# Expert products and sums over both column halves at once, row scaling split between ScalarE and VectorE

## What is computed

```python
logits = x @ router_w + router_b
topk_vals, topk_idx = top_k(logits, 2)
full_w = sum(one_hot(topk_idx, 8) * softmax(topk_vals)[..., None], axis=-2)
h = einsum('td,edf->etf', xf, expert_w) + expert_b[:, None, :]     # 8 dense experts
combined = einsum('etf,te->tf', silu(h), full_w)
y = x + combined @ proj_w + proj_b
return norm_w * (y / sqrt(mean(y * y, -1) + 1e-6))
# around it: x = x + 0.5 * ffn(layernorm(x))
```

## Time and profile before

| | us |
|---|---|
| median of 3 runs | 890.74 |
| lowest, highest | 890.63, 891.22 |
| the profiled execution | 892.65 |
| its span, first to last instruction | 890.8 |
| TensorE (PE) busy | 822.6, 92% |
| VectorE (DVE) busy | 701.0, 79% |
| GpSimd (POOL) busy | 585.2, 66% |
| ScalarE (ACT) busy | 521.4, 59% |
| mean granted TensorE clock | 0.971 |

### The profile page before, as it was taken

The page is one execution under the profiler, slowest core; times in us unless marked ns, Lnnn a source line. Parts: engine busy times, 40 slices in busy tenths (PEclk is TensorE's granted clock), DMA queues, the critical chain, the costliest instruction groups (busy, mean ns, idle before and its releaser), DMA issues. The chain is left out here.

```text
span 890.8 us, 17017 instructions
## 1 busy us (share of the span) xinstructions
PE 822.6 (92%) x4848; PEld 724.0 (81%) x4848; DVE 701.0 (79%) x1824; ACT 521.4 (59%) x1252; POOL 585.2 (66%) x444
## 2 busy tenths in 40 slices
PE   5998888767999999999999999999999998999984
PEld 4776776656889999999999899899999986787873
DVE  6899989899776776776866867767767797789987
ACT  3654534445765765755865766756767663554542
POOL 3667746368587687777777787777777812556743
PEclk9999988978999999999999999999999999899998
DMA  8053153410212311312312312212212100000001
GB/s 302 1 178 105 72 201 142 142 36 12 49 24 59 106 24 35 94 35 59 94 24 47 94 24 71 85 33 47 71 41 54 25 1 29 1 1 24 24 1 47
DMA packets 26673, 55.98 MB, mean 63 GB/s; under 512 B 3568, under 2 KB 9840, under 8 KB 25104
## 3 DMA queue, kind: packets, MB, share of 16 engines
q1 hardware_dynamic: 26640, 55.59, 21.4%
HBM read 22.02 MB, written 12.58 MB: 39 GB/s over the span
## 5 line engine op out<-in xcount | busy, mean ns | idle before, releaser
L1050 POOL TENSOR_TENSOR at_ql<-at_rot,at_qh 128x512 fp32r<-128x512 f32 x62 | 79.8, 1287 | 99.6 <-ACT at_qh L1272 99.6
L1289 ACT ACTIVATE at_pr<-at_sm,at_low 128x512 f32<-128x512 f32 (+3 forms) x256 | 140.4, 555 | 0.9 <-DVE at_low L1137 0.8
L1295 ACT ACTIVATE at_pth<-at_pt 128x512 fp32r<-128x512 f32 (+1 forms) x192 | 95.8, 525 | 76.0 <-PE at_pt L1449 75.2
L603 ACT ACTIVATE f_s<-f_ex,f_cols 128x512 f32<-128x512 f32 x128 | 84.1, 686 | 86.0 <-PE f_ex L751 46.3
L293 POOL TENSOR_TENSOR f_acc<-f_acc,f_u 128x512 f32<-128x512 f32 x68 | 100.8, 1509 | 40.8 <-DVE f_u L482 27.7
L1147 DVE TENSOR_SCALAR at_pr<-at_pr,at_inv 128x128 f32<-128x128 f32 (+3 forms) x256 | 113.1, 504 | 2.3
L1137 DVE CUSTOM_DVE_ANT_0 at_sm<-at_sc,at_mask 128x512 f32<-128x512 f32 (+3 forms) x256 | 109.8, 484 | 2.5 <-issue 2.4
L1152 DVE TENSOR_TENSOR at_ptl<-at_pt,at_pth 128x512 fp32r<-128x512 f32 (+1 forms) x192 | 108.7, 593 | 1.7 <-ACT at_pth L1295 1.5
L1059 POOL TENSOR_TENSOR at_rot<-ga,cos 128x512 f32<-128x512 f32 x78 | 104.2, 1336 | 4.1 <-POOL at_ql L1050 2.4
L1065 POOL TENSOR_TENSOR at_rot<-at_rot,gc 128x512 f32<-128x512 f32 x78 | 101.5, 1301 | 8.1 <-POOLq L1082 2.1
L1449 PE MATMUL at_pt<-ident,at_pr 128*128 128x128 f32 x640 | 96.3, 278 | 9.3 <-DVE at_pr L1147 6.8
(11 more groups left out here) (212 smaller groups left out, 2262.7 us busy)
## 6 DMA issues: line engine op xcount, KB each, us to landing
gc<-ga SPq DMA_DIRECT2D x160, 128.0 KB, 2.3
ga<-in_attn_w SPq DMA_DIRECT2D x4, 1280.0 KB, 7.7
attn_split<-gb SPq DMA_DIRECT2D x4, 1280.0 KB, 9.6
attn_split<-gc SPq DMA_DIRECT2D x4, 1280.0 KB, 12.1
gb<-attn_split SPq DMA_DIRECT2D x8, 512.0 KB, 4.2
at_wo<-attn_split SPq DMA_DIRECT2D x8, 512.0 KB, 4.3
x<-in_x SPq DMA_DIRECT2D x4, 512.0 KB, 9.0
e_raw<-in_expert_w SPq DMA_DIRECT2D x8, 256.0 KB, 6.7
```

The costliest lines, as they stand in the source:

```text
L1289: act.activation(pr[h % 2][:, cols], sm[h % 2][:, cols], ACT.Exp, bias=low[h % 2][:, i:i + 1], scale=-1.0, accum_out=tot[h % 2][:, i:i + 1 ...
```

## The change

The rings `s_ring` and `u_ring` become two wide buffers of both halves each, with the same capacity. One product of 1024 columns (the bank of `w_ps` is read twice by a broadcast) takes the place of two, except for expert 7 of the last block. The pair sums, GpSimd's sums, the rounding of the sum and its rest become one operation each. The semaphores count up by two at once. Row scaling is divided: ScalarE multiplies each row by its inverse root mean square (four operations after silu of expert 3), VectorE then multiplies all four tiles by `norm_w` in one operation, after expert 4 and `z_rest`. GpSimd's `add_rows` moves from behind the sum of expert 3 to behind the pair of experts 4 and 5.

```diff
@@ -116,8 +116,8 @@
         fw = sb("fw", [P, BT, P])
         wT = sb("wT", [P, SEQ], F32R)
 
-        s_ring = [sb(f"s{n}", [P, SEQ]) for n in range(4)]
-        u_ring = [sb(f"u{n}", [P, SEQ]) for n in range(4)]
+        s_ring = [sb(f"s{n}", [P, C, SEQ]) for n in range(2)]
+        u_ring = [sb(f"u{n}", [P, C, SEQ]) for n in range(2)]
         acc = sb("acc", [P, C, SEQ])
         ch, cl = sb("ch", [P, C, SEQ], F32R), sb("cl", [P, C, SEQ], F32R)
 
@@ -157,7 +157,7 @@
         step_ps = t_ps + w_ps + w_ps
         RING = len(ex_ps)
         SILU0 = RING
-        MULT0 = len(s_ring)
+        MULT0 = C * len(s_ring)
         X0 = 1
 
 
@@ -282,30 +282,25 @@
                 if first:
                     scale_queries(i)
                 for j, e in enumerate(SUMS if more else SUMS[:2]):
-                    for f in range(C):
-                        n = C * e + f
-                        if e < 4:
-                            pool.wait_ge(mult_done, MULT0 + C * E * i + n + 1)
-                        else:
-                            pool.wait_ge(pair_done, PAIRS * i + C * (e // 2 - 2) + f + 1)
-                        if j > 0:
-                            pool.wait_ge(acc_done, ACC * i + C * (j - 1) + f + 1)
-                        pool.tensor_tensor(acc[:, f, :], acc[:, f, :], u_ring[n % 4][:], ALU.add).then_inc(acc_done, 1)
+                    if e < 4:
+                        pool.wait_ge(mult_done, MULT0 + C * E * i + C * e + C)
+                    else:
+                        pool.wait_ge(pair_done, PAIRS * i + C * (e // 2 - 2) + C)
+                    if j > 0:
+                        pool.wait_ge(acc_done, ACC * i + C * j)
+                    pool.tensor_tensor(acc[:], acc[:], u_ring[e % 2][:], ALU.add).then_inc(acc_done, C)
                     if e == 3:
                         residual(i + 1)
-                        if prev:
-                            add_rows(i - 1)
+                    if e == 5 and prev:
+                        add_rows(i - 1)
                 if not more:
 
-                    for f in range(C):
-                        e3, e4 = (u_ring[(C * e + f) % 4] for e in (3, 4))
-                        pool.wait_ge(mult_done, MULT0 + C * E * i + C * 4 + f + 1)
-                        pool.tensor_tensor(e4[:], e4[:], e3[:], ALU.add).then_inc(acc_done, 1)
-                    for f in range(C):
-                        e4 = u_ring[(C * 4 + f) % 4]
-                        pool.wait_ge(mult_done, MULT0 + C * E * i + C * 5 + f + 1)
-                        pool.wait_ge(acc_done, ACC * i + C * 2 + f + 1)
-                        pool.tensor_tensor(e4[:], e4[:], last5[:, f, :], ALU.add).then_inc(acc_done, 1)
+                    e4, e3 = u_ring
+                    pool.wait_ge(mult_done, MULT0 + C * E * i + C * 4 + C)
+                    pool.tensor_tensor(e4[:], e4[:], e3[:], ALU.add).then_inc(acc_done, C)
+                    pool.wait_ge(mult_done, MULT0 + C * E * i + C * 5 + C)
+                    pool.wait_ge(acc_done, ACC * i + C * 2 + C)
+                    pool.tensor_tensor(e4[:], e4[:], last5, ALU.add).then_inc(acc_done, C)
                     add_rows(i - 1)
 
             if first:
@@ -398,27 +393,26 @@
                 dve.tensor_tensor(lo, e_raw[:, e, :], hi.bitcast(F32), ALU.subtract).then_inc(e_lo_done, 1)
 
             def sum_rest(i):
-                for f in range(C):
-                    dve.wait_ge(chi_done, C * i + f + 1)
-                    dve.tensor_tensor(cl[:, f, :], acc[:, f, :], ch[:, f, :].bitcast(F32), ALU.subtract).then_inc(clo_done, 1)
+                dve.wait_ge(chi_done, C * i + C)
+                dve.tensor_tensor(cl[:], acc[:], ch[:].bitcast(F32), ALU.subtract).then_inc(clo_done, C)
 
             def add_sixth(f):
 
-                e6, e7 = s_ring[(C * 6 + f) % 4], s_ring[(C * 7 + f) % 4]
+                e6, e7 = (s[:, f, :] for s in s_ring)
                 dve.wait_ge(mult_done, MULT0 + C * E * LAST + C * 7 + f + 1)
-                dve.tensor_tensor(e7[:], e7[:], e6[:], ALU.add).then_inc(pair_done, 1)
+                dve.tensor_tensor(e7, e7, e6, ALU.add).then_inc(pair_done, 1)
 
             def add_middle(f):
 
-                e7 = s_ring[(C * 7 + f) % 4]
+                e7 = s_ring[1][:, f, :]
                 dve.wait_ge(pair_done, PAIRS * LAST + 2 * f + 1)
-                dve.wait_ge(acc_done, ACC * LAST + C * 3 + f + 1)
-                dve.tensor_tensor(e7[:], e7[:], u_ring[(C * 4 + f) % 4][:], ALU.add).then_inc(pair_done, 1)
+                dve.wait_ge(acc_done, ACC * LAST + C * 3 + C)
+                dve.tensor_tensor(e7, e7, u_ring[0][:, f, :], ALU.add).then_inc(pair_done, 1)
 
             def last_rest():
                 for f in range(C):
                     dve.wait_ge(chi_done, C * BATCH + f + 1)
-                    dve.tensor_tensor(cl_last[:, f, :], s_ring[(C * 7 + f) % 4][:], ch_last[:, f, :].bitcast(F32),
+                    dve.tensor_tensor(cl_last[:, f, :], s_ring[1][:, f, :], ch_last[:, f, :].bitcast(F32),
                                       ALU.subtract).then_inc(clo_done, 1)
 
             def add_last_residual(t):
@@ -441,10 +435,8 @@
                 dve.tensor_scalar(ms[:], ss[:], 1.0 / D, RMS_EPS, ALU.mult, ALU.add).then_inc(rms, 1)
 
             def scale_rows(i):
-                dve.wait_ge(rr_done, i + 1)
-                for t in range(BT):
-                    dve.scalar_tensor_tensor(out=y[:, t, :], in0=y[:, t, :], scalar=rr[:, t:t + 1], in1=n_w,
-                                             op0=ALU.mult, op1=ALU.mult).then_inc(xn_done, 1)
+                dve.wait_ge(yr_done, BT * i + BT)
+                dve.tensor_tensor(y[:], y[:], n_w.unsqueeze(1).to_broadcast([P, BT, D]), ALU.mult).then_inc(xn_done, BT)
 
             def group_rest(i, half):
                 part = slice(half * GW // 2, (half + 1) * GW // 2)
@@ -467,23 +459,26 @@
                     expert_rest(5)
                 group_at = (3, 6) if more else (2, 3)
                 for e in range(E):
-                    for f in range(C):
-                        n = C * e + f
-                        dve.wait_ge(silu_done, SILU0 + C * E * i + n + 1)
-                        if f == 0:
-                            dve.wait_ge(sel_done, E * i + e + 1)
-                        if e in (3, 4) or more and e in (5, 7):
-                            dve.wait_ge(acc_done, ACC * i + C * (3 if e == 7 else e - 3) + f + 1)
-                        if more and e == 6:
-                            dve.wait_ge(pair_done, PAIRS * i + f + 1)
-                        to = acc[:, f, :] if e == 0 else u_ring[n % 4][:]
-                        if not more and e >= 5:
-                            to = last5[:, f, :] if e == 5 else s_ring[n % 4][:]
-                        dve.tensor_tensor(to, s_ring[n % 4][:], w_ps[e % 2][:], ALU.mult).then_inc(mult_done, 1)
-                        if not more and e == E - 1:
+                    slot, to = s_ring[e % 2], acc if e == 0 else u_ring[e % 2]
+                    if not more and e >= 5:
+                        to = last5 if e == 5 else slot
+                    narrow = not more and e == E - 1
+                    dve.wait_ge(sel_done, E * i + e + 1)
+                    if e in (3, 4) or more and e in (5, 7):
+                        dve.wait_ge(acc_done, ACC * i + C * (3 if e == 7 else e - 3) + C)
+                    if more and e == 6:
+                        dve.wait_ge(pair_done, PAIRS * i + C)
+                    if narrow:
+                        for f in range(C):
+                            dve.wait_ge(silu_done, SILU0 + C * E * i + C * e + f + 1)
+                            dve.tensor_tensor(slot[:, f, :], slot[:, f, :], w_ps[e % 2][:], ALU.mult).then_inc(mult_done, 1)
                             if f > 0:
                                 add_middle(f - 1)
                             add_sixth(f)
+                    else:
+                        dve.wait_ge(silu_done, SILU0 + C * E * i + C * e + C)
+                        dve.tensor_tensor(to[:], slot[:], w_ps[e % 2][:].unsqueeze(1).to_broadcast([P, C, SEQ]),
+                                          ALU.mult).then_inc(mult_done, C)
                     if e == 0 and prev:
                         mean_square(i - 1)
                     if e == 0 and prev and (more or first):
@@ -493,17 +488,16 @@
                         expert_rest(7)
                         dve.wait_ge(e_hi_done, E + 1)
                         dve.tensor_tensor(p_lo[:], p_raw, p_hi[:].bitcast(F32), ALU.subtract).then_inc(p_split, 1)
-                    if e == 2 and prev:
-                        scale_rows(i - 1)
                     if e == 4 and (more or first):
                         z_rest(i + 1)
+                    if e == 4 and prev:
+                        scale_rows(i - 1)
                     if e == 4 and not more:
                         sum_rest(i)
                     if more and e in (5, 7):
```

(22 more changed lines are left out.)

2 lines of the change are left out of this document (1 added, 1 removed).

## The result

The changed kernel is slower: 903.26 us median of 4 runs (901.55 to 904.36) against 890.68 (890.57 to 891.22) beside it, a ratio of 1.0138 with a 95% interval of 1.012 to 1.0156. The forecast was 888.1 and the range ended at 893.0. The profiled execution took 901.55 us, the fastest of the four, while that of the kernel before, at 892.65, lay 1.9 above its median.

What follows compares the result with a forecast made beforehand. Loop blocks were taken as bound by a chain alternating between VectorE and GpSimd. Gains of 1.7 - 2.2 + 1.7 + 0.8 + 0.1 + 2 x 0.25 = 2.6 us took the median from 890.74 to 888.1; range 884.5 to 893.0.

Steps and rivals of the forecast that it cites:

- the gate: From the last pair sum to the gate weights in F1's loop blocks: taken as 4.1 us.
- The rule that the forecast quoted: VectorE and GpSimd: whichever issues first holds the shared pair; a wide sum raises the longest hold from 1.35 to 2.39.
- The chain up to the last pair, F2: Second feed-forward's loop block, rebuilt: last pair ends at 814.9 against 815.04, a gain of 0.15 us.
- the wide sum back to back: GpSimd's sum of 1024 columns: 2.35 us each in a run, against 2.7 for two narrow ones.
- The chain, F1: First feed-forward's loop block, rebuilt: last pair ends at 82.0 against 83.7, gaining 1.7 us in each of two.
- The second rival's order: First feed-forward: GpSimd's residual gets in ahead of the scaling, losing 1.2 in each of two blocks; 890.5, chance 0.27.
- One low grant of 2.2 us: After F1's first loop block, a TensorE wait of 2.1 to 3.6 us brings a low clock, costing 2.2 us.
- F1's last block: Product of expert 5 ends 0.8 us earlier and releases the selection before TensorE's last half expert: gain 0.8.
- The wide product's 1.13 net: VectorE's product of 1024 columns: 1.13 us, against 1.20 for two narrow ones; bounds 1.05 to 1.20.
- TensorE's wait at a selection in F1's loop blocks: Sign in the profile: TensorE's waits at L762 of about 0 in the first feed-forward's loop blocks.
- The slower rival: Some 4 us wait ahead of the last half expert, low clock behind adds 2.05; 892.6, 0.22 shared with wide forms without gain.
- The rival that wide forms give nothing: Wide forms take two narrow ones' time (1.20, 2.7), losing up to 1.8 a loop block; 891 to 893, shared chance 0.22.

Runs made afterwards that it cites:

- the one-input form: The changed kernel with the gate's difference written as four operations with one SBUF input and a per-partition scalar: 893.88 us, ratio 1.0025 to the kernel before.
- the kernel with narrow sums: The changed kernel with GpSimd's five sums of a block as two narrow operations each: 896.07 us, ratio 1.0043 to the kernel before.
- The busy matmuls: The changed kernel with six unread matmuls ahead of TensorE's wait for gate weights, in blocks after each feed-forward's first: 894.31 us, ratio 1.0031.
- the narrow kernel: The kernel before with the new scaling, and GpSimd's addition to x moved behind the next block's gate: 881.68 us, ratio 0.9895.

## Why the prediction was wrong

**The step that failed: the gate.** The forecast took it as fixed, 4.1 us from the last pair to the restart of TensorE, in both feed-forwards. It was 4.05 before in F2's first loop block (815.04 to 819.09) and 5.02 in the changed kernel (818.14 to 823.16), and 5.02 in F1's (85.09 to 90.11). The rule that the forecast quoted, that a VectorE operation with two SBUF inputs waits out one GpSimd instruction, was right, and the trace bore it out. It was applied to the large operations only. The gate's difference has two SBUF inputs too, and a moved boundary of GpSimd's last sum catches it: a narrow sum ended 0.2 us after it was asked, the wide one ran 1.7 us longer. A list of every such operation, of any size, with the GpSimd instruction under way beside it, would have shown this. Price: up to 1.1 us a block and 5.3 to 5.6 in all, by the one-input form, about half of the 11.6 us between the forecast of the profiled span (888.2) and its measured 899.8.

**The chain up to the last pair, F2.** Forecast 814.9, against 815.04 before: 27.4 us after the restart. It came at 28.52 (818.14 - 789.62). Of the 1.1 us, 0.58 arose ahead of GpSimd's first sum, which started 9.08 us after the restart and not 8.5, since the product ahead of it started at 7.71 and not at 7.2 (0.20 of that was a wait for its selection). Another 0.45 arose at the three sums, 7.50 against 7.05. The second and the third had their products long before (VectorE's ended at 799.68 and 802.74); they started 2.54 us apart and not 2.35, as each waited for the sum ahead of it, which writes the same `acc`. The six narrow sums in the same place of the kernel with narrow sums take 7.55. The same is seen in F1's first block, where two narrow sums take 2.50 from start to start:
```profile
32.08 2.41 POOL L291 TENSOR_TENSOR f_acc<-f_acc,f_u 128x1024 f32<-128x1024 f32 x1 [0.17 <-POOL f_acc L291]
```
```profile
29.84 5.04 POOL L293 TENSOR_TENSOR f_acc<-f_acc,f_u 128x512 f32<-128x512 f32 x4 [9.51 <-DVE f_u L482]
```
The first line is the changed kernel (its sums start at 29.51, 32.08 and 34.66), the second the kernel before. The forecast's 2.7 for two narrow sums came from a run of four that VectorE's old scaling disturbed (5.41 against 5.04 here), so a wide sum in a chain gains nothing. The residual passed the delay on (it ended 18.92 after the restart, forecast 18.0), the scaling and the addition after it. The failed terms are the wide sum back to back, 2.35 that measured 2.54, and a start of the chain that was taken from the kernel before. F1's first block, forecast unchanged, lost 1.66: its difference began 0.77 later (25.59 after the restart against 24.82) and was held like the others.

**The chain, F1.** Forecast: pair at 82.0, 1.7 us earlier than before. It came at 85.09, or 32.25 us after the restart against 31.66 before and 29.92 forecast. The second rival's order happened:
```profile
71.88 3.46 DVE L439 TENSOR_TENSOR f_y<-f_y,f_rows 128x1024 f32<-128x1024 f32 x1
...
71.87 2.40 POOL L256 TENSOR_TENSOR f_zres<-z,f_rows 128x1024 f32 x1
```
The two started within 0.01 us of each other and GpSimd won. That rival was priced at 1.2 us a block. The other 1.1 were there before: the third sum ended 19.06 us after the restart, forecast 18.07. Most of that is the clock again. The wait of 1.97 us ahead of this block, to which the first block's held difference adds, was followed by 3.4 us at half clock, and the second residual sum came 5.41 us after the restart, against 4.46 before (56.54 - 52.08):
```profile
58.25 0.69 DVE L430 TENSOR_TENSOR f_y<-f_wide,f_zres 128x512 f32<-128x512 f32 x1 [0.69 <-PE f_wide L772]
```
With the rival's order the forecast would have been 890.5. The gate in six of eight blocks, the chain in F2 and a part of the clock lie between that and the profiled 901.55; the rest up to the median of 903.26 is open.

**The clock.** One low grant of 2.2 us was forecast, after a wait of 2.1 to 3.6. In fact waits of 1.97, 3.50, 1.85 and 2.25 us for the gate weights and of 2.21 and 3.68 for a selection were each followed by 0.50 for about 3.4 us, and waits of 1.73 and 2.11 by none. The kernel before had a wait of 2.47 that kept the full clock, one of 2.60 until 72.23 that didn't (0.50 from 71.8 to 75.2), and falls of 6.8 us in places. So the places were wrong: the forecast put one new fall behind one long wait, while shorter waits brought falls too, and the long falls before F1's last block and in it became shorter. The net size, at most 1.8 us by the sums above, is close to the 2.2 forecast by luck.

**What was right.** The wide product's 1.13 net, and the wide sum's 2.4 where it stands alone. That the division of the scaling is a gain; but alone it gave 0.7 a block in F1, where the loop blocks were to gain 1.7 each by the whole change. In F1's last block 1.82 us were gained against 0.8 forecast, and all of it can be the clock's, as half clock took 13.6 us of that block before and 6.8 in the changed kernel. Attention moved by 0.6 of 573. ScalarE's scaled copies cost 0.43 each in F2 (1.70 for four) against 0.40, beside other work.

**What was wrong beside it.** TensorE's wait at a selection in F1's loop blocks was to go to about 0. It was 2.21 and 2.11 us against 2.60 and 2.47 before:
```profile
76.53 0.59 PE L761 MATMUL f_wide<-f_wT,f_pick 128*128 128x512 f32 x1 [2.21 <-DVE f_u L480]
```
The wait for product 4 did go, as that product ended at 70.7. A wait for product 5 took its place, which stands behind the held scaling (75.27 + 1.21). The slower rival told a long wait ahead of the last half expert with a low clock behind it. That sign was seen in F1 (3.68 us until 151.59, half clock from 151.9), but the block got shorter, and the loss lay elsewhere; the rival stopped at 892.6. The rival that wide forms give nothing was right for the sums in a chain, though not by its numbers, and not for the products, which have their 1.13 against 1.20; the later start behind whole sums and the longer hold take more than that gives.

**What stays open.** Why wide products alone cost 1.3% where under wide sums they cost nothing is explained for two thirds of one block's loss by the waits for whole sums, and at most 1.8 of the 8.6 us that its eight blocks grew by can be the clock's (30.6 us at half clock against 27.1). The rest is open. The busy matmuls weren't tried in the kernel before. The 3.6 us by which the medians are further apart than the two profiles aren't explained. What decides whether a wait of about 2.2 us is followed by a low grant is open too.

## What to carry to other kernels

Before an operation of one engine is made wider, list every operation of the other engine that these traces show held beside it (those with two SBUF inputs, and the cast), the 128x4 ones on the critical path first, and see which one a longer instruction now covers. Widening saved little here (0.07 us a product on VectorE; on GpSimd nothing in a chain of sums, 2.54 to 2.58 against 2.50) and coarsens each hand-off that it stands in; it pays only where nobody waits for the first half. Take the price of the narrow form where nothing disturbs it. Where TensorE waits some 2 us for a result, the wait may be followed by a low clock: fill it with matmuls nobody reads and measure, and move long GpSimd work to where VectorE runs operations with an input in PSUM.

## What the runs showed of the hardware

- An operation of 128x4 with two SBUF inputs was held for up to 1.5 us by a 2.39 us GpSimd operation (1.74 against 0.28), and the same arithmetic in four operations with a scalar operand took 0.58 in all at the same place.
- A VectorE cast of 128x8, with one input, was held too: 0.66 us beside a narrow GpSimd sum and 0.58 beside a wide one, each time to that sum's end, against 0.17 alone.
- Wide GpSimd sums into the same buffer started 2.54 to 2.58 us apart and two narrow ones took 2.50, though a wide one lasts 2.40 and two narrow ones 2 x 1.29.
- Half clock for some 3.4 us followed waits of TensorE as short as 1.85 us, and of two waits of 2.18 and 2.19 us one brought it and the other didn't.
- Six idle-time matmuls a block took the changed kernel from 1.010 to 1.014 down to 1.003, and similar ones the narrow kernel from 0.9895 to 0.9835.
